# The second layer's experts of one group dealt out over the whole chain of the next group

## What is computed

```
x = x + attn(layernorm(x))            # stage E: rms norm, 8-bit activations, ternary weights,
                                      #   16 heads of 16, causal; its output projection likewise
x = x + cross(layernorm(x), ctx)      # stage F: 16 heads, 361 context rows of 128
x = x + moe(layernorm(x))             # stage G:
def moe(x):                           # 8 experts and a shared one, 256 -> 128 -> 256
    scores = softmax(x @ gate_w.T); keep and renormalise the best two
    y  = sum_e (gelu(x @ Wg[e]) * (x @ Wu[e]) * cw[:, e]) @ Wd[e]
    sh = (gelu(x @ sWg) * (x @ sWu)) @ sWd
    return y + sh
```

## Time and profile before

| | |
|---|---|
| median of three runs | 1668.27 us (1666.18 to 1669.59) |
| profiled execution | 1667.32 us, span 1665.6 us |
| PE, DVE busy | 1284.8 us (77%), 1008.3 us (61%) |
| ACT, POOL busy | 513.7 us (31%), 413.2 us (25%) |
| granted TensorE clock, mean | 0.861 |
| transfers | 122.42 MB, 73 GB/s |

### The profile page before, as it was taken

The page is one execution under the profiler, slowest core; times in us unless marked ns, Lnnn a source line. Parts: engine busy times, 40 slices in busy tenths (PEclk is TensorE's granted clock), DMA queues, the critical chain, the costliest instruction groups (busy, mean ns, idle before and its releaser), DMA issues.

```text
span 1665.6 us, 24431 instructions
## 1 busy us (share of the span) xinstructions
PE 1284.8 (77%) x7936; PEld 886.7 (53%) x7936; DVE 1008.3 (61%) x2148; ACT 513.7 (31%) x1269; POOL 413.2 (25%) x528
## 2 busy tenths in 40 slices
PE   2678877878783999952659878689787697986988
PEld 1455644645543566631347654367554575545755
DVE  4457577566563233327668675768657686676852
ACT  2233323324231222201216422246113362233630
POOL 1132234335152100026522112221213212032100
PEclk9688878978896999985769989679898798997998
DMA  9510100390105111111225210144100450104501
GB/s 373 210 47 1 32 16 8 108 382 21 57 18 213 53 45 45 42 39 47 98 45 115 64 40 12 35 90 99 41 12 1 101 122 16 25 11 88 118 7 43
DMA packets 69692, 122.42 MB, mean 73 GB/s; under 512 B 25404, under 2 KB 55100, under 8 KB 68032
## 3 DMA queue, kind: packets, MB, share of 16 engines
q1 hardware_dynamic: 63936, 110.04, 22.0%
q0 software_dynamic: 5632, 10.77, 2.3%
HBM read 67.69 MB, written 53.07 MB: 73 GB/s over the span
## 4 chain that ended last, share of the span: by engine, by line
PE 39%; issue 31%; DVE 10%; POOL 9%; POOLq 3%; DVEq 3%; ACT 2%; DMA 2%; SPq 1%; another core or an unknown queue 0%; ACTq 0%
PE ps L1150 7%; PE ps L1169 3%; PE ps L1323 3%; PE ps L1397 3%; PE ps L1339 3%; PE ps L526 2%; POOL experts L1792 2%; PE ps L1309 2%; PE ps L534 2%; POOL headbd L682 2%; PE ps L1068 1%; PE ps L1046 1%; PE ps L595 1%; PE ps L1410 1%; PE ps L1057 1%
## 5 line engine op out<-in xcount | busy, mean ns | idle before, releaser
L1638 ACT ACTIVATE probs<-ps,small 100x361 f32<-100x361 f32 x256 | 141.5, 558 | 94.9 <-DVE small L2372 89.4
L2372 DVE TENSOR_REDUCE small<-ps 100x2 f32<-100x722 f32 x128 | 115.7, 907 | 37.5 <-PE ps L1309 37.3
L1150 PE MATMUL ps<-every,xT_t 128*128 x256 | 121.7, 599 | 0.4 <-issue 0.4
L1397 PE MATMUL ps<-hT,experts 128*128 128x400 f32 x288 | 115.1, 550 | 1.2 <-DVE small L731 1.2
L1323 PE MATMUL ps<-cst,probs 100*121 100x100 f32 x768 | 104.7, 272 | 7.8 <-DVE probsT L2380 7.4
L1323 PEld LDWEIGHTS ps<-cst,probs 100*121 100x121 f32 x768 | 95.2, 186 | 22.3 <-issue 13.5
L2380 DVE TENSOR_SCALAR probsT<-ps 121x600 f32<-121x600 f32 x128 | 99.2, 775 | 9.8 <-PE ps L1323 9.8
L1339 PE MATMUL ps<-probsT,values_ 121*32 121x100 f32 x1536 | 91.3, 254 | 0.9 <-DVE probsT L2380 0.9
L1309 PE MATMUL ps<-k_stack,q_stack 96*100 96x362 f32 x256 | 82.4, 403 | 6.4 <-ACT probs L1638 5.7
L1199 PE MATMUL ps<-identb,xq 100*128 100x100 bf16 x128 | 13.6, 242 | 88.2 <-DVE y L2247 50.1
L1397 PEld LDWEIGHTS ps<-hT,experts 128*128 128x128 f32 x288 | 59.0, 213 | 41.2 <-issue 12.0
(11 more groups left out here) (328 smaller groups left out, 2896.0 us busy)
## 6 DMA issues: line engine op xcount, KB each, us to landing
k_stack<-key_d SPq DMA_DIRECT2D x192, 90.5 KB, 3.2
tok_d<-wt SPq DMA_DIRECT2D x1, 14848.0 KB, 45.7
res_d<-wt SPq DMA_DIRECT2D x1, 14848.0 KB, 42.8
every<-e_d SPq DMA_DIRECT2D x8, 1536.0 KB, 15.4
ctxT<-ctxT_d SPq DMA_DIRECT2D x8, 726.0 KB, 4.3
key_d<-k_hi SPq DMA_DIRECT2D x32, 181.0 KB, 2.8
key_d<-k_lo SPq DMA_DIRECT2D x32, 181.0 KB, 3.2
gates<-gate_d SPq DMA_DIRECT2D x28, 200.0 KB, 4.4
```

The costliest lines, as they stand in the source:

```text
L1150: ins = e.matmul(ps[:, 2 * i + t % 2, :], xT_t[:, t % 2, c, :], every[:, bass.ds(base + (i * DC + c) * HID0, HID0)], start=(c == 0), stop= ...
L1397: ins = e.matmul(bank(2 * i + j % 2, n=NT), w[:, c, :], hT[:, c, :], start=(c == 0), stop=(c == DC - 1))
L1638: ins = e.activation(f_e[:, n % 2, i, 0:LC], bank(2 * (n % 2) + i, S, LC), ACT.Exp, bias=h_nm[:, n % 2, i:i + 1], accum_out=h_sum[:, b, h: ...
L2372: inc(e.tensor_reduce(h_nm[:, n % 2, 0:2], ps[0:S, 2 * (n % 2):2 * (n % 2) + 2, 0:LC], AX, ALU.max, negate=True), "F_nm")
```

## The change

`self_*` is gone; stage E uses `attend` of the first layer with a prefix for its semaphores, also for group 0. `before_e` gives the second half banks 4 and 5, `after_e` works in bank 4 + h alone. The experts move to banks 0 to 3: one pair for gate and up products (0 and 1, no alternation), down products in 2 and 3. Their input `hTG`, gates and hidden values move to space of weights that the first layer needed, and the residual is kept in `xall` in place of `x`; so the wait `x_free` falls, and the output is written by `tokens_out` within the next group's key transfers. The hardware loops are unrolled.

The order: `chain(g + 1)` is `before_e` of both halves (positions 0 to 17), two empty pieces, `attend` (20 to 38) and `after_e` of both halves (39 to 56). `dealt` puts one step of `experts_g(g)` behind each of 12 positions:

| position | 1 | 2 | 4 | 8 | 9 | 13 | 17 | 23 | 28 | 33 | 41 | 47 |
|---|---|---|---|---|---|---|---|---|---|---|---|---|
| PE: gate_up | 0 | 1 | | | 2 | 3 | 4 | 5 | 6 | 7 | 8 | |
| PE: down | | | 0 | | 1 | 2 | 3 | 4 | 5 | 6 | 7 | 8 |
| DVE: hidden | 0 | gates | | 1 | 2 | 3 | 4 | 5 | 6 | 7 | 8 | `G_acc` |

```diff
+GATED_AT = (1, 2, 4, 8, 9, 13, 17, 23, 28, 33, 41, 47)
+def both(first, second, rounds):
+    for _ in range(rounds):
+        for st in (first, second):
+            next(st, None)
+            yield
+def dealt(chain, extra, at):
+    for i, _ in enumerate(chain):
+        if i in at:
+            next(extra)
...
-            feed(NG - 1)
+            feed(0, True)
+            for g in range(NG - 1):
                 W(e, "F_kvp", g, 5 * NB)
                 e.dma_start(ctxT[:], ctxT_d[g + 1]).then_inc(ld["ctxT3"].sem, 16)
                 spread_gates(g)
-                W(e, "G_acc", g)
-                e.dma_start(out_d[g], x[:]).then_inc(ld["out"].sem, 16)
-                e.wait_ge(ld["out"].sem, g * 16 + 16)
-                e.sem_inc(x_free.sem, 1)
+                feed(g + 1)
...
             def group_pe(g, last=False):
-                W(e, "E_kT", g, 1, 1)
-                W(e, "E_v", g, 1, 1)
-                self_pe(e, "E_", g)
-                in_turn(after_e(g, 0), after_e(g, 1))
...
                 if last:
-                    in_turn(experts_g(g))
+                    list(experts_g(g))
                 else:
-                    in_turn(late(before_e(g + 1, 1)), before_e(g + 1, 0), experts_g(g))
+                    dealt(chain(g + 1), experts_g(g), GATED_AT)
+                    W(e, "G_acc", g)
...
+                def gate_up(j):
+                    if j:
                         W(e, "G_hid", g, j)
+                    for i in range(2):
+                        o = EXPERT_AT[j] * W1 + i * DC * HID1
+                        w = experts[:, o:o + DC * HID1].rearrange("p (c n) -> p c n", c=DC)
+                        for c in range(DC):
+                            ins = e.matmul(bank(i, n=NT), w[:, c, :], hTG[:, c, :],
+                                           start=(c == 0), stop=(c == DC - 1))
+                    inc(ins, "G_h")
...
+                gate_shift_dve(e, NB, g1_shifted, g)
+                hidden(0)
+                yield
+                e.wait_ge(g1_e.sem, g1_e.at(g))
+                gate_top_dve(e, NB, True, gates_all[:], probs[:, 0, 0:NB * 64], probs[:, 1, 0:NB * 64])
+                e.sem_inc(names["G_top"].sem, 1)
+                yield
+                yield
+                for j in range(1, E1):
+                    hidden(j)
                     yield
...
-            with e.Fori(0, NG - 1) as g:
+            for g in range(NG - 1):
                 group_dve(g)
             group_dve(NG - 1, True)
```

More of the change, by code:

```diff
@@ L882, in feed @@
                 keys_in(g, 1, 0)
+                if not first:
+                    tokens_out(g - 1)
                 for b in range(1, NB):
@@ new lines, in down @@
+                def down(j):
+                    W(e, "G_hid", g, j + 1)
+                    o = (EXPERT_AT[j] + 1) * W1
+                    for b in range(NB):
+                        if j == 0 and b == 2:
+                            W(e, "G_gT", g)
+                        ins = e.matmul(ps[0:S, 2 + b // 2, (b % 2) * D:(b % 2 + 1) * D],
+                                       g_hid[:, j % 2, b * S:(b + 1) * S],
+                                       experts[:, o - D:o], start=(j == 0 and b % 2 == 0), stop=(j == E1 - 1 and b % 2 == 1))
+                    inc(ins, "G_o")
@@ L1414, in experts_g @@
+                gate_up(0)
+                yield
+                gate_up(1)
+                yield
+                W(e, "G_top", g)
+                inc(e.transpose(ps[0:NB * 8, 3, 0:S], gates_all[:].rearrange("p b n -> p (b n)"), identS), "G_gTp")
+                down(0)
+                yield
+                yield
+                for j in range(2, E1):
+                    gate_up(j)
+                    down(j - 1)
                     yield
-            with e.Fori(0, NG - 1) as g:
+                down(E1 - 1)
@@ L1527, in behind @@
                 yield
-                yield from attend(g)
+                yield from attend("C_", g)
                 for h in range(2):
@@ L1653, in group_act, with act @@
                 if last:
-                    in_turn(experts_g(g))
+                    list(experts_g(g))
                 else:
-                    in_turn(late(before_e(g + 1, 1)), before_e(g + 1, 0), experts_g(g))
+                    dealt(chain(g + 1), experts_g(g), GATED_AT)
             def experts_g(g):
-                e.wait_ge(g1_shifted.sem, g1_shifted.at(g))
-                e.activation(g_e[:, 0:NB, :], g_e[:, 0:NB, :], ACT.Exp).then_inc(g1_e.sem, 1)
-                for j in range(E1):
+                def act(j):
                     W(e, "G_h", g, j + 1)
@@ L1843, in group_pool @@
                 if not last:
-                    in_turn(late(before_e(g + 1, 1)), before_e(g + 1, 0))
-            with e.Fori(0, NG - 1) as g:
+                    list(chain(g + 1))
+            for g in range(NG - 1):
                 group_pool(g)
@@ L2064, in behind @@
                 yield
-                yield from attend(g, ways)
+                yield from attend("C_", g, ways)
                 yield
@@ L2388, in group_dve, with hidden @@
                 if last:
-                    in_turn(experts_g(g))
+                    list(experts_g(g))
                 else:
-                    alternating(before_e(g + 1, 0), late(before_e(g + 1, 1)), experts_g(g))
+                    dealt(chain(g + 1), experts_g(g), GATED_AT)
             def experts_g(g):
-                gate_shift_dve(e, NB, g1_shifted, g)
-                e.wait_ge(g1_e.sem, g1_e.at(g))
-                gate_top_dve(e, NB, True, gates_all[:], probs[:, 0, 0:NB * 64], probs[:, 1, 0:NB * 64])
-                e.sem_inc(names["G_top"].sem, 1)
-                for j in range(E1):
+                group = xall[:, bass.ds(g * NB, NB), :]
+                def hidden(j):
                     W(e, "G_act", g, j + 1)
```

452 lines of the change are left out of this document (195 added, 257 removed).

## The result

The changed kernel is slower: 1726.14 us, median of four runs (1723.46 to 1739.15), against 1668.93 us for the kernel before in the same runs (1666.18 to 1670.88); the ratio is 1.036, with an interval of 1.0304 to 1.0415. Forecast were 1714 us and a range of 1650 to 1742. The profiled execution took 1723.46 us with a span of 1721.8.

What follows compares the result with a forecast made beforehand. PE was 77% busy, with holes and a swinging clock in the second layer; DVE bounds the new first part. Weaves +36, group 0 +6, last experts +8, unrolling -4 sum to +46: median 1714 us, range 1650 to 1742.

Steps and rivals of the forecast that it cites:

- The weaves: Second layer, first expert matmul of group g to first cross-attention score of g+1, three times: 423 against 386.9, +36 us.
- group 0's attention: Second layer, group 0's self attention, alone in the new form: 40.1 + 1.5 against 35.6, +6 us.
- the last experts: Last group's experts, alone: gates about 5 us later, steps 4.75 instead of 4.4; together +8 on 48.5 us.
- 53, 50 and 38: Forecast us for a weave's parts: first part with fewer experts, attention with three experts, `after_e` with the ninth.
- The four stalls: First part of a weave: DVE idle before hidden(0), (2), (3) and (4) for 2.5, 3.0, 3.4 and 1.9 us.
- full price: An expert step in a queue where PE has no hole costs 4.4 us, read from the last group.
- Rival 3: First part of the weave: clock falls like `after_e`'s 0.63, +5 us a weave; with uncovered table loads 1742 to 1760; chance 0.09.
- The table loads: ACT in the weaves: 24 more Exp/Gelu loads of 1.28 us, charged nothing; if uncovered up to 31 us, in upper end.
- Unrolling: -4 forecast: `after_f` takes 15.5 us in the hardware loop and 13.8 outside; three times about 1.4, -4 us.
- The experts fill the holes: Rival 1, faster: PE 87% busy over the weave, 109 us each, total 1618; break-even 1.7 us an expert; chance 0.19.
- Half absorbed: Rival 2: an expert costs 1.9 to 2.6 us, weaves 127 to 133, total 1672 to 1690; chance 0.12.
- 29 us of holes: PE idle in the third weave, busy 95.0 of 124.5 us; 15.7 of it in `after_e`, 6.0 in the attention.

Runs made afterwards that it cites:

- the first experiment: Changed kernel plus a one-column Exp on ScalarE behind the last Gelu (position 47), loading the Exp table early: 1709.85 us, ratio 1.0181.
- the best changed form: Changed kernel with early Exp, no expert in the attention, and DVE's steps for experts 2, 3 and 4 later: 1682.09 us, ratio 1.0073.

## Why the forecast held, and where it did not

Term by term, in the profiled executions, the changed kernel is 56.1 us longer where the forecast's sum has 46. The weaves are 1.9 above their term, what lies between them and the experts behind them 14.4, group 0's attention is 5.5 under its term and the last experts 0.7. That the sum came out only 10 us short is partly luck: the 6 us for group 0, which were not lost, cover more than a third of what was missed between the weaves.

**The weaves, 141 forecast, 141.6 measured.** Each term stood: 53, 50 and 38 against 54.9, 49.7 and 37.1. The method was to price an expert by its place: full price where PE is solid, DVE's part and the stalls where the chain waits for DVE. The experiments bear this out, 3.6 to 4.1 us in the attention (4.4 was the full price), 2.6 in `after_e`, and 4 to 5 us of removable stalls in the first part. The attention had little room: PE is busy 91% of its middle and 31.0 of 37.6 us over the whole of it, before anything is put in.

**What was off within them.** The four stalls were counted at 10.8 us and are 14.9, since I priced gate_up(2) and (3) at the upper clock (2.9 us) although rival 3 of the forecast says that the clock would be low there; it was 0.72 over the part and 0.53 and 0.56 in these products. The rest of the part is 54.9 - 14.9 = 40.0 us, counted at 41.7, so of the 4.1 too few in the stalls 1.7 were hidden by work counted too high. Rival 3 is thus true as a mechanism: the two products take 5.0 us more than at the upper clock, and it has +5 a weave. That the weave still came out at 141.6 is because other terms were counted too high, and that too is luck.

**The table loads were charged at nothing, and this is the step that failed.** The forecast looked for an exposed load among the ten in the weave and priced it at up to 1.28 us. It did not ask which table is in place when the weave ends. One load of the ten is exposed, the last, and with the clock behind it costs 4.3 us a group, 13 together, which the first experiment gave back. (The stage grew by 10.2 and not 13, since the kernel before had one cross attention of 74.4.) Of the other loads nothing is seen in the sums, the attention came out at 49.7 for 50 with six of them in it; they were not tried one by one. The Trainium skill ("ScalarE: Activation LUTs", section "What ACT_TABLE_LOAD costs") has load and drain together at 2.66 us for a switch. This trace does not show that drain, and the price would not explain the 4.3 us: the first Exp begins 1.29 us after the load does, at 1571.48.

**Unrolling: -4 forecast.** The -4 was for `after_f`, read as 15.5 us in the loop and 13.8 outside. 15.5 is the longest of the loop's; the unrolled kernels have it between 13.4 and 15.6 too, and three times it takes 44.0 us in the changed kernel for 43.9 before. This term was read from one case, and nothing of it came. The pauses at the jumps were rightly left in the weaves. The experiment shows 16.7 us for the unrolling, the greater part of it at other places than these pauses. Since I compared weaves with the measured 386.9, which includes 13 of it, the total did not suffer; but that unrolling alone makes a faster kernel, and that the rest of the diff loses 72 us and not 56, stood nowhere. The Trainium skill ("Runtime: NRT & Kernel Launch", section "Instruction fetch mechanics") says that a taken branch whose target is outside the pages already fetched makes the engine fetch that page before it can go on, and gives this as one reason why kernels prefer unrolling where possible. This case's runs agree with the preference, with 1.3% for it; that the fetch is the reason, no run here shows.

**The last experts, +8 forecast, +7.3 measured.** The sum is right, its division is not. It was 5 for the late gates and 3 for the longer steps. The experiment that undoes both gets 6.3 back, but the single pair alone makes 7.0 in the old kernel, whose gates are chosen as early as before. The steps were sized right (4.81 us for 4.75); the single pair also holds the products at the start, and the late gates add little to that (57.0 against 56.2).

**Group 0's attention, +6 forecast.** From the first score to the last value it is 38.7 us, from 34.0 before: +4.7. The score it begins with comes 1.6 us earlier, its `after_e` is 1.6 shorter and its `after_f` 1.0, so only +0.5 is left by the first expert. `after_e` with one bank a half was not looked at.

**The rivals.** The result lies within the forecast's own range, 1690 to 1742. *The experts fill the holes* failed at the point that the forecast gave for it: its break-even was 1.7 us an expert, and no order reached less than 2.6 over the weave. *Half absorbed*, 1672 to 1690 with weaves of 127 to 133, is where the best changed form is, at 1682 with 130.7.

## What to carry to other kernels

Before spreading work over a longer chain, measure what one piece costs at each place; a stage in which PE is already busy 31.0 of 37.6 us takes it at nearly full price, and averages over the chain (here 29 us of holes) promise what no place gives. When activation functions are mixed, look at the table that is in place where the next stage starts, and load it early where ACT is idle: here one instruction took the ratio from 1.036 to 1.018. When a diff does several things, run each alone: the best kernel of this case, 1654 us, is the old one with its loops unrolled, a part of the diff that was credited with 4 us.

## What the runs showed of the hardware

An exposed table load of 1.28 us left PE waiting for 1.76 us and at the lower clock (0.52) for the next 10.1 us, although it was busy for 9.26 of them; hence 4.3 us lost, in six cross attentions of six. In four others, with no such load, the clock at that place was 0.68, and 2.4 us were lost. Eight products of 128x128 by 400 took 2.85 us at clock 1.00, and 5.55 and 5.15 at 0.53 and 0.56, where PE had paused ahead of them. A hardware loop's two jumps showed as gaps of 2 us each on PE, and the attentions right behind them were 4.5 us longer together; unrolling gave 16.7 us altogether, of which the rest was not traced to a jump. In a stage of nine experts a step took 4.81 us with one pair of banks and 4.42 with two, and the whole stage 56.2 us for 49.2.
